# Two-layer metaformer block: where the first expert layer's gate is applied, and the order around it

## The reference

```python
logits = tokens @ router_w.T
probs = softmax(logits)
rw, re = top_k(probs, 2)
rw = rw / max(rw.sum(-1), 1e-12)
combine = zeros((N, 8)).at[arange(N)[:, None], re].set(rw)
out = tokens
for e in range(8):
    h = gelu(tokens @ w1[e] + b1[e])
    y = h @ w2[e] + b2[e]
    out = out + combine[:, e:e + 1] * y
```

## Time and profile before

| | |
|---|---|
| median of 3 runs | 769.71 us (768.87 to 771.29) |
| profiled execution | 768.34 us, span 766.5 us |
| busy share of the span | PE 73%, PE's weight loads 61%, DVE 51%, ACT 42%, POOL 51% |
| dense stage | 193.3 to 399.2 us |
| POOL in the dense stage | 107.06 us busy of 205.9 |
| DVE in the dense stage | 73.38 us busy of 205.9 |

### The profile page before, as it was taken

The page is one execution under the profiler, slowest core; times in us unless marked ns, Lnnn a source line. Parts: engine busy times, 40 slices in busy tenths (PEclk is TensorE's granted clock), DMA queues, the critical chain, the costliest instruction groups (busy, mean ns, idle before and its releaser), DMA issues.

```text
span 766.5 us, 16046 instructions
## 1 busy us (share of the span) xinstructions
PE 561.3 (73%) x5352; PEld 464.2 (61%) x5353; DVE 390.8 (51%) x1109; ACT 321.8 (42%) x761; POOL 389.0 (51%) x445
## 2 busy tenths in 40 slices
PE   0559999976579799999984688335399989999000
PEld 0347777755357577767762466125299989999000
DVE  4856777738472702530046165575655544555521
ACT  0737888871344344552134211222155545555000
POOL 4477999933055676673333000575377007730673
PEclk9999999996599899999995599555599999999555
DMA  8323333324062333331930000012044334442421
GB/s 330 97 63 88 83 94 85 95 77 199 4 210 85 122 130 126 124 112 54 297 101 0 1 1 0 34 53 65 21 125 144 96 97 118 133 115 74 126 81 53
DMA packets 81257, 74.97 MB, mean 98 GB/s; under 512 B 9068, under 2 KB 74820, under 8 KB 80684
## 3 DMA queue, kind: packets, MB, share of 16 engines
q1 hardware_dynamic: 76588, 64.72, 26.5%
q0 software_dynamic: 4608, 9.45, 4.3%
HBM read 50.92 MB, written 23.63 MB: 97 GB/s over the span
## 4 chain that ended last, share of the span: by engine, by line
PE 52%; POOL 16%; DVE 16%; issue 7%; ACT 5%; DMA 3%; SPq 0%; POOLq 0%; DVEq 0%; ACTq 0%
PE bank L743 12%; PE bank L804 8%; PE bank L689 7%; PE bank L705 7%; PE bank L754 6%; POOL gathered_or_att L512 5%; POOL padded_or_w L503 4%; POOL gathered_or_att L571 4%; POOL gathered_or_att L521 3%; PE bank L661 3%; PE bank L259 3%; DVE normed L1029 2%; DVE ln_stats L1007 2%; PE bank L734 1%; PE bank L703 1%
## 5 line engine op out<-in xcount | busy, mean ns | idle before, releaser
L547 POOL TENSOR_TENSOR padded_or_w<-padded_or_w,gathered_or_att 128x384 f32<-128x384 f32 x96 | 95.7, 1006 | 100.4 <-ACT padded_or_w L903 75.5
L559 POOL DMA_INDIRECT sorted_x<-normed,slot x72 | 70.4, 978 | 111.5 <-DVE slot L1196 90.1
L571 POOL DMA_INDIRECT gathered_or_att<-sorted_y,slot x72 | 69.1, 960 | 94.7 <-DMA sorted_y<-padded_or_w 73.3
L903 ACT ACTIVATE padded_or_w<-bank,moe_b 128x384 f32<-128x384 f32 x96 | 55.3, 580 | 119.0 <-PE bank L689 118.9
L705 PEld LDWEIGHTS bank<-moe_or_conv,padded_or_w 128*128 128x128 f32 x576 | 79.8, 196 | 29.1 <-issue 8.3
L689 PE MATMUL bank<-chan_major,moe_or_conv 128*128 128x384 f32 x192 | 81.8, 512 | 2.4 <-ACT padded_or_w L903 2.4
L705 PE MATMUL bank<-moe_or_conv,padded_or_w 128*128 128x128 f32 x576 | 82.4, 281 | 0.0
L1225 DVE TENSOR_TENSOR att_or_moe<-att_or_moe,bank 128x256 f32<-128x256 f32 x104 | 43.7, 420 | 57.1 <-PE bank L754 42.5
L917 ACT ACTIVATE att_or_moe<-bank 128x256 f32<-128x256 f32 x104 | 39.9, 383 | 64.3 <-PE bank L743 63.7
L259 PE MATMUL bank<-consts,normed 128*128 128x128 f32 x144 | 34.2, 373 | 42.1 <-DVE normed L1029 35.4
L743 PE MATMUL bank<-att_or_moe,chan_major 128*128 128x128 f32 x416 | 56.4, 280 | 11.0 <-DVE chan_major L1217 11.0
(11 more groups left out here) (166 smaller groups left out, 1059.0 us busy)
## 6 DMA issues: line engine op xcount, KB each, us to landing
gathered_or_att<-combine SPq DMA_DIRECT2D x24, 768.0 KB, 4.0
padded_or_w<-windows SPq DMA_DIRECT2D x192, 48.0 KB, 2.0
sorted_x<-zeros SPq DMA_DIRECT2D x26, 256.0 KB, 4.4
padded_or_w<-sorted_x SPq DMA_DIRECT2D x26, 256.0 KB
sorted_y<-padded_or_w SPq DMA_DIRECT2D x26, 256.0 KB, 2.4
padded_or_w<-in_moe_w SPq DMA_DIRECT2D x1, 4096.0 KB, 12.1
residual<-in_x_tok SPq DMA_DIRECT2D x2, 1152.0 KB, 6.3
out<-residual SPq DMA_DIRECT2D x12, 192.0 KB, 2.2
```

Source lines behind the costliest of these rows:

```text
L547: nc.gpsimd.tensor_tensor(HB[n % DRING], HB[n % DRING], GB_[k % 3][:, n % 4, :], ALU.mult).then_inc(S("gated"), 1)
L559: nc.gpsimd.indirect_dma_start(xs_dram[b], bass.IndirectOffsetOnAxis(ap=POS[b][:, k, t:t + 1], axis=0), TN[b][:, t, :], None).then_inc(S(f ...
L571: nc.gpsimd.indirect_dma_start(G[k][:, t, :], None, ys_dram[b], bass.IndirectOffsetOnAxis(ap=POS[b][:, k, t:t + 1], axis=0)).then_inc(S(f" ...
L903: nc.scalar.activation(HB[n % DRING], banks[HBANK[n % 2]][:, 0:DG], ACT.Gelu, bias=B1C[:, e:e + 1]).then_inc(S("gelu"), 1)
```

## The change

The gate is no longer multiplied onto the GELU's output. DVE applies it, per token and so per partition, to the second product as it adds that to the residual. POOL's part, SP's broadcast transfers and their three buffers go. Eight experts can no longer accumulate in one bank, because each has another gate. So each step's second product gets a bank of its own, in turn, and the bias product another: nine slots a round (`y_slot`), 108 in all, on the same two banks. The products wait until DVE has read slot - 2. `DLAG` and `DRING` go from 4 and 5 to 3 and 4, and the gates of both images are kept. Some phases stand elsewhere in the list: the square roots of the layer norms directly behind them, and the product and square root of each group norm one step behind its sums.

```diff
-    DLAG, DRING = 4, 5
+    DLAG, DRING = 3, 4
...
+        SLOTS = NB * NG * (EX[0] + 1)
+
+        def y_slot(n):
+
+            return n + n // EX[0]
+
...
-        order += spread(0, 4, [])
-        order += [("RC", 0, 0), ("RE", 0, 0), ("RX", 0), *groups("YA", 1), ("LN", "LR", 0, 1)]
-        order += spread(4, half + DLAG, [
-            (7, ("SQ", "LR", 0, 1)), *every(10, 1, groups("RT", 0, 1)), *every(12, 4, groups("AN", "LR", 0, 1)),
+        order += spread(0, 3, [])
+        order += [("RC", 0, 0), ("RE", 0, 0), ("RX", 0), *groups("YA", 1), ("LN", "LR", 0, 1), ("SQ", "LR", 0, 1)]
+        order += spread(3, half + DLAG, [
+            *every(10, 1, groups("RT", 0, 1)), *every(12, 4, groups("AN", "LR", 0, 1)),
             (17, ("RC", 0, 1)), (19, ("RE", 0, 1)), (33, ("RX", 1))])
-        order += [("LN", "XL", 0)]
+        order += [("LN", "XL", 0), ("SQ", "XL", 0)]
...
-            (65, ("XC", 0)), (66, ("XCE", 0), ("GN", "XC", 0)), (69, ("GS", "XC", 0)), (71, ("GQ", "XC", 0)), (73, ("XCH", 0)),
-            *every(75, 1, taps(0, 0, 54)), (93, ("GN", "XM", 0)), (95, ("GS", "XM", 0)), (97, ("GQ", "XM", 0)), (98, ("XMH", 0))])
+            (65, ("XC", 0)), (66, ("XCE", 0), ("GN", "XC", 0)), (67, ("GS", "XC", 0)), (67, ("GQ", "XC", 0)), (73, ("XCH", 0)),
+            *every(75, 1, taps(0, 0, 54)), (93, ("GN", "XM", 0)), (94, ("GS", "XM", 0)), (94, ("GQ", "XM", 0)), (98, ("XMH", 0))])
...
-            for k in range(10):
-                gates(k)
             combine_rows(1)
-            for k in range(10, 4 * NG):
-                gates(k)
...
-            def dense(n):
-                if n < DN:
-                    k = n // 4
-                    pool.wait_ge(S("gelu"), n + 1)
-                    if n % 4 == 0:
-                        pool.wait_ge(S(f"gates{k % 3}"), 16 * (k // 3 + 1))
-                    nc.gpsimd.tensor_tensor(HB[n % DRING], HB[n % DRING], GB_[k % 3][:, n % 4, :], ALU.mult).then_inc(S("gated"), 1)
...
-                    acc = banks[YBANK[gg % 2]]
-                    pe.wait_ge(S("gated"), n + 1)
-                    if e == 0:
+                    slot = y_slot(n)
+                    acc = banks[YBANK[slot % 2]]
+                    pe.wait_ge(S("gelu"), n + 1)
+                    if slot >= 2:
+                        pe.wait_ge(S("y_read"), slot - 1)
+                    for t in range(TG):
+                        ins = nc.tensor.matmul(acc[:, t * P:(t + 1) * P], HB[n % DRING][:, t * P:(t + 1) * P], W2E[:, e, :], start=True, stop=True)
+                    ins.then_inc(S("y_used"), 1)
+
+                    if e == EX[0] - 1:
                         if g == 0:
                             pe.wait_ge(S(f"comb_rows{b}"), 16)
...
+                        pe.wait_ge(S("y_read"), slot)
+                        nc.tensor.matmul(banks[YBANK[(slot + 1) % 2]][:, 0:DG], CMT[b][0:ROWS, g, :], B2D[:, :],
+                                         start=True, stop=True).then_inc(S("y_used"), 1)
...
+                slot = y_slot(n - DLAG)
+                if g == 0 and e == 0:
                     dve.wait_ge(S(f"normed_added{b}"), NG)
-                dve.wait_ge(S("y_used"), EX[0] * (gg + 1))
+                    dve.wait_ge(S("comb_set"), b + 1)
+                if slot:
+                    dve.wait_ge(S("y_read"), slot)
+                dve.wait_ge(S("y_used"), slot + 1)
+                acc = banks[YBANK[slot % 2]]
+                for t in range(TG):
+                    xt = XT[b][:, g * TG + t, :]
+                    ins = nc.vector.scalar_tensor_tensor(xt, acc[:, t * P:(t + 1) * P], COMB[b][:, g, e, t:t + 1], xt, ALU.mult, ALU.add)
+                ins.then_inc(S("y_read"), 1)
+                if e == EX[0] - 1:
+                    added(gg, slot + 1)
```

55 lines of the change are left out of this document (20 added, 35 removed).

## The result

The changed kernel took 793.79 us in the median of 4 runs (792.68 to 800.19), beside 770.50 for the kernel before, measured with it: a ratio of 1.0317, 95% interval 1.0255 to 1.0379. It is slower, by 23.3 us in the medians and by 25.4 in the spans of the two profiled executions (766.5 and 791.9 us). Forecast were 800.0 us, with a range of 786 to 815, and a growth of 30.3. Every ratio in this document is one of fast runs to fast runs of the kernel before in the same session, whose median lay between 770.5 and 774.4 us.

A forecast was written before the change was run, and what follows sets the result against it. PE's work plus its waits was taken to bound the dense stage. Waits behind DVE's blocks, 6.2 + 6.1 + 10.6 + 2.1 + 5.3 = 30.3 us, gave 798.6 us for the execution and 800.0 for the median, range 786 to 815.

The forecast's parts named there:

- 1, tiles of image 1: Normalisation of image 1, on DVE before step 3: PE idles about 10 us and restarts at a low clock, +6.2 us.
- 2, routing: Routing of image 1, behind step 17: PE idles 10.1 us and loses 2.4 to the clock, +6.1 us.
- 3, copies: Copies of the gates at step 33, two short DVE operations: 0 us.
- 4, tiles of image 0: Normalisation of image 0, behind step 50: PE idles 9.0 us and loses 2.4 to the clock, +10.6 us.
- 5, first group norm: First group norm, step 66: PE waits 1.7 us, then 1.25, with no clock loss, +2.1 us.
- 6 and the end: Second group norm, step 93, and the last steps, whose second products follow DVE at 0.98 us each: +5.3 us.
- three idle stretches of 9 to 10 us: Sign in PE's stage: three such waits ended by DVE's new line, each restart at clock 0.5.
- The new operation: DVE's 288 gated additions, three per step: 0.30 us each, 0.98 us a step, a DVE round below PE's 11.5.
- The rival in which DVE bounds every round: At 0.45 us per gated addition a DVE round takes 12.4 us, over PE's 11.5: 811 us, chance 0.12.
- the rule of the Trainium skill that was weighed: A PSUM source costs DVE 62 cycles more, 65 ns per operation; left out, it would add some 2 us.
- Routing without POOL: Image 1's routing takes 6.65 us, not 14.1, once POOL is idle; rival that it stays slow: 807 us, chance 0.03.
- The rival on the faster side: DVE's blocks fit under PE's lead, so only gains remain: 13.3 us less, 756.4 us, chance 0.03.

The follow-up runs named there:

- Experiments 5 to 7: Changed kernel with one ungated addition per step (ratio 1.0295), then with more accumulator banks (1.0294), then with DVE's blocks cut one after another (1.0249 to 0.9974).
- experiment 5: Changed kernel with one plain ungated 128x384 addition per step in place of three gated ones: ratio 1.0295, stage 234.9 us.
- experiment 2: Kernel before without gates, POOL's multiplications and the broadcast transfers left out: ratio 0.987, stage 203.1 us.
- experiment 3: Kernel before with all of POOL's multiplications but only the first three of 24 broadcast transfers: ratio 0.9978, stage 211.8 us.
- experiment 4: Changed kernel with one extra POOL multiplication per step whose result nobody reads: ratio 1.0301, stage 234.4 us.
- experiment 1: Kernel before with only the changed order of the square roots and the group norms' products: ratio 1.0086, stage 214.8 us.
- experiment 9: Image 0's gates by DVE as in the changed kernel with pieces and three banks, image 1's by POOL as before: 763.32 us, ratio 0.9888.
- experiment 8: Kernel before with image 1's routing two steps later, behind the addition it held up: ratio 0.9921, stage 205.2 us.
- experiment 7: Changed kernel with DVE's blocks cut in succession: image 0's tiles, image 1's tiles, routing in pieces, more banks; ratios 1.0249, 1.0169, 0.9974, 0.9974.
- e6_tiles_image0: Changed kernel with image 0's 18 normalised tiles one per step and the first convolution some steps later: ratio 1.0249, stage 228.2 us.
- e7_tiles_both: Changed kernel with both images' normalised tiles one per step and image 1's routing behind step 24: ratio 1.0169, stage 222.2 us.

## Why the prediction was right, point by point

| place | forecast | measured | how it came |
|---|---|---|---|
| 1, tiles of image 1 | +6.2 | +5.9 | ym 6 |
| 2, routing | +6.1 | +4.9 | ym 6 to ym 27 |
| 3, copies | 0 | 0.1 | ym 27 to ym 48 |
| 4, tiles of image 0 | +10.6 | +10.3 | ym 48 to ym 64 |
| 5, first group norm | +2.1 | +1.4 | ym 64 to ym 90 |
| 6 and the end | +5.3 | +4.9 | behind ym 90 |
| stage | 30.3 | 27.4 | |
| outside it | 0 | -2.1 | -1.3 ahead, -0.8 behind |

The forecast growth of 30.3 us is 7.0 over the 23.3 of the medians: 2.9 lie in the stage and 2.1 outside it, where the start of the stage moves by more than that from run to run (191.3 to 196.2 us), and the last 2.1 are how the profiled executions lie to the medians.

The mechanism stands: blocks of DVE's other work became waits of PE, since a bank now serves a step. Experiments 5 to 7 show it from three sides. A third of DVE's new work taken away gives 1.7 us, more banks 4.8, and the same work in another order 25.0 (236.7 to 211.7). Only the end was not taken apart: its 4.9 us stayed in every reordered kernel with DVE's gates for image 1, and experiment 5 alone shortened it, by 1.0.

- **The signs that the prediction named.** The stage grew from 205.9 to 233.9 us (about 236 was said), its busy time by 6.4 (some 5), and a round without blocks stayed at 11.5. Of the three idle stretches of 9 to 10 us only routing's came so, with 9.82. The other two were 6.49, with 1.07 and 1.95 of waiting for ACT just ahead. PE did not get further ahead than two slots for that: the block's end, which sets when it goes on, came as forecast.

- **The new operation.** Forecast were 0.30 apart and 0.98 us a step, measured are 0.29 (six in 1.76) and 0.87. Every block is 0.1 shorter for it: from its first addition to PE's next product it is 1.00 us (223.49 to 224.49) for the forecast's 1.1. The end is not: the last five steps' additions take 4.9 us (420.82 to 425.74) for 5.0, and its 0.4 less is that the second norm was done about 5.5 us behind ym 90 and not 5.95. The rival in which DVE bounds every round fell. By the rule of the Trainium skill that was weighed (VectorE: DVE Perf Modes, the TRN2 errata), a step would have been 1.17; no run here shows its surcharge on a PSUM source.
- **Place 1** came out right although the idle time was off. PE idled 1.07 and 6.49 us, not 10: it had done its steps ahead of the block at the lower clock (1.48 us for an operation of 0.83), and DVE's block began and ended 1 us earlier from the start of the span, as the stage did. Neither changes the sum, because the block's end sets ym 2: it came 32.4 us behind the first product, forecast 32.3. The 0.3 less is the restart, 2.1 for 2.4.
- **Place 2** is the term that was mis-sized most, by 1.2 us. The idle time was 9.82 us for 10.1, and the loss behind it 1.6 for 2.4: ym, hid, ym, hid from 263.18 to 267.38 take 4.2 us where they take 2.64 in the earlier trace rows, and the stretch shows 0.68 for a clock where the other two restarts show 0.53 and 0.50. A restart is no constant: at places 1, 2 and 4 it cost 2.1, 1.6 and 2.5 us.
- **Routing without POOL** was read from two rows only, and held: 6.65 us. Experiments 2 and 3 show that POOL's multiplications cause the 14.1. The Trainium skill's rule (SBUF — State Buffer, two separate sides) agrees with both halves, the slow small operations of SBUF in experiment 3 and the gated additions from PSUM in experiment 4. A tensor_scalar with one tensor input was slowed too (0.18 to 0.92 us). The prediction's short form of the rule, two SBUF inputs, does not cover that; the section names a second kind beside it, a DVE operation in a 2-port perf mode, and whether this tensor_scalar ran in one, no run here shows.
- **Place 5** was near by luck. I took no clock loss because 1.7 us of idling is nearer 0.80 than 3.97. Experiment 1 has just 1.70 there, and lost 3 us to the clock behind it; the changed kernel, with 1.39, lost none. The range had that case in it.
- **The rival on the faster side** priced the gains at 13.3 us. The runs show 6.4 for routing, none for ACT's stalls, which stay (1.95 at 315.27), and 2 to 6 at ym 0. The last is in part the bias product's move to the end of the round. From the transposes of image 0's gates to ym 0 it takes 9.2 us in experiment 2, without gates but with the bias in front (1.6 us at the lower clock), and 7.5 in the changed kernel and in experiment 9. Ahead of those transposes experiment 2 is another 1.3 us longer, and that is mostly chance: the kernel before takes 13.5 us there and experiment 8, the same up to that point, 14.5.
- **The order itself** I costed at nothing apart from its place in DVE's blocks. In the kernel before it costs 0.86% (experiment 1); what it costs the changed kernel was not measured.

## What to carry to other kernels

An accumulator that collects a whole round hides what the reader does meanwhile. Split it per step, and a block on the reading engine that is longer than banks times step (here 2 x 1.32 us) becomes a wait, though that engine is busy for only 60% of the stage. Before such a change list the blocks in the reader's queue and cut or move them first. Then ask of each part of the program which engine has cover there: here a kernel that gave half of the steps to each waited for neither. And a wait found in the profile (3.97 us) may be worth more by moving one phase than the redesign that happens to remove it.

## What the runs showed of the hardware

- This is DVE beside POOL's 128x384 operations of 1.0 us, experiment 3 against experiment 2. From where POOL resumes (252.78) a tensor_tensor on SBUF rows of 144 goes from 0.31 to between 0.65 and 1.09 us, and one of 18 columns from 0.18 to between 0.62 and 1.03. The first three, while POOL stood still, keep their 0.31; a reduction stays at 0.30 and a reciprocal at 0.27 throughout. The gated additions from PSUM kept their mean of 345 ns with POOL busy for 108 of 234 us (experiment 4). So not every operation pays.
- The length of a wait does not tell by itself whether PE's clock falls behind it. After 1.70 us it fell to 0.50 (experiment 1). After the same wait of 1.95 us for ACT, at the same place, it stayed at 1.00 in the changed kernel, where only one product follows before the next wait, and in the first run of experiment 7 (e6_tiles_image0), where PE then works for 8 us without a stop:

```profile
315.30:316.60 1.30, 0.88 (x2) 0.27 (x2) 1.30 (x4) 0.77 (x2) 0.88 (x2) 1.00 0.00 0
```

```profile
314.50:322.50 8.00, 8.00 (x47) 6.25 (x48) 5.56 (x22) 3.90 (x8) 1.66 (x2) 1.00 0.01 2
```

In the second run of experiment 7 (e7_tiles_both) the same 1.95 us were followed by a clock of 0.56, and the first product took 1.39 us in place of 0.91:

```profile
311.90:314.00 2.10, 2.10 (x7) 1.55 (x8) 0.51 (x2) 0.97 (x2) 0.00 (x0) 0.56 0.91 279
```

What decides it stays open.
